# First layer of a four-layer graph network: one copy instruction in place of two, and another order of turns

## The chip, the cores and the metric

The kernel runs on one core of one Trainium2 chip. The metric is the device time of one execution in microseconds (us), which is the time that the core needs from its first to its last instruction and what lies around it.

## The reference

Eight graphs of 1024 nodes with 256 features each pass through four layers, one after the other. Each layer is a kind of attention over the 1024 x 1024 adjacency of the graph. Only the first layer is touched by the change:

```
feat_proj = feats @ fc_w.T + fc_b
q = feat_proj @ q_w.T + q_b                      # one number for each node
k = feat_proj @ k_w.T + k_b                      # one number for each node
logits = q + transpose(k)                        # 1024 x 1024
masked = logits + (1.0 - adj) * -1e9
masked = where(masked >= 0, masked, 0.01 * masked)   # leaky
out = softmax(masked, axis=-1) @ feat_proj + feats
```

The second layer is an attention with one head and a layer norm. The third and the fourth are attentions with eight heads, and the fourth has a feed-forward part with a GELU behind it. All numbers are float32 where this text has to do with them.

## The kernel before

One engine program is written by hand for each engine, and semaphores order the engines among each other. All engines loop over the eight graphs (seven in a hardware loop, the last one unrolled behind it). Within one graph the stages follow each other: first layer, second layer, the two layers with heads, feed-forward. The end of a graph's feed-forward part also holds the beginning of the next graph's first layer.

The first layer goes over T = 8 tiles of 128 rows. For tile t:

- GpSimd (`penalties`, L1311) writes (adj - 1) * 1e9 into `scores[t % 3]`. It waits until TensorE has transposed tile t - 3, because the ring has three buffers.
- VectorE adds the row of keys and takes the row maximum (L1076), and makes the negated maximum with three small instructions (L1078, L1080, L1082). This step is called the maxima here.
- ScalarE makes `slack[t % 2]`, 0.01 times the scores with a bias (L824). This is the slack pass.
- VectorE takes the larger of scores + q and slack (L1089). This is the leaky pass.
- ScalarE takes the exponential in place and sums the row (L829), and signals `p_ready`.
- TensorE (`attend`) transposes the eight 128 x 128 blocks of the tile into PSUM banks 4 and 5 (L536). I write T(t) for these eight instructions. Both banks belong to one tile, so T(t) waits for the copies of tile t - 1.
- ScalarE copies bank 4 (L780) and VectorE copies bank 5 (L969) into `probs_t[t % 2]`.
- TensorE multiplies the copied tile with the values (L546, 16 instructions). I write AV(t) for these. The result lies in bank 6 + t % 2.
- VectorE divides by the row's sum, adds x, and writes `y` (L1095 and L1100). I write y(t) for L1100.

The order of TensorE is T(0), T(1), AV(0), T(2), AV(1), ..., T(7), AV(6), AV(7), both before and after. In its step t VectorE does the maxima of tile t, the leaky pass of tile t - 1, the copy of tile t - 2 and y(t - 3). In its step t ScalarE does the slack pass of tile t, the exponential of tile t - 1 and the copy of tile t - 2. START = 3 of these steps are done ahead, during the feed-forward part of the graph before; they hold three maxima, three slack passes, two leaky passes and two exponentials.

When the first layer is done, TensorE turns `y` (L471) for the second layer's products (L500). The feed-forward part ends with products at L492 and additions of VectorE at L1246.

Of the kernel before, what the change touches and what calls it, by code (L numbers as in the profile page):

```python
# [21 lines left out]
ACT = mybir.ActivationFunctionType  # L22
ALU = mybir.AluOpType
# [4 lines left out]
D = 256  # L28
T = N // P
C = D // P  # L30
HALF = 512
# [55 lines left out]
DVE_STEPS_START = 10  # L87
START = 3

# [8 lines left out]
def build(nc, a, out):  # L98
    B = out.shape[0]
    with ExitStack() as ctx:  # L100
# [3 lines left out]
        def sem(name):  # L104
# [156 lines left out]
        per_graph += [(s, 16 * H) for s in max_row_in] + [(s, 64 * H) for s in o_moved]  # L261
        per_graph += [(s, T) for s in (pen_ready, mask_used, s_done, slack_done, leaky_done, y_ready, g_ready,
                                       e_ready, g3_ready)]
        per_graph += [(s, 2 * T) for s in (s_ready, p_ready, t_done, t_act, t_dve, av_done, av_taken, normal)]
        per_graph += [(s, 2 * H) for s in (max_cast, rows_done, rows_taken, v_ready, o_out)]
# [176 lines left out]
        def _(pe):  # L442
# [84 lines left out]
            def attend(b, layer, t):  # L527

                base = b * 2 * T + layer * T
                if t < T:  # L530
                    pe.wait_ge(p_ready, base + t + 1)

                    pe.wait_ge(t_act, base + t)
                    pe.wait_ge(t_dve, base + t)
                    for k in range(T):
                        last = nc.tensor.transpose(flat[:, 4 * HALF + k * P:4 * HALF + (k + 1) * P],  # L536
                                                   scores[:, t % 3, k * P:(k + 1) * P], ident[:, :])
                    last.then_inc(t_done, 1)
                if t > 0:
                    pe.wait_ge(t_act, base + t)  # L540
                    pe.wait_ge(t_dve, base + t)
# [214 lines left out]
        def _(act):  # L756
# [18 lines left out]
            def copy_probs(b, layer, t):  # L775
# [42 lines left out]
            act.wait_ge(const_made, CONSTS)  # L818
            def layer0(b, steps):

                for t in steps:
                    if t < T:
                        act.wait_ge(s_ready, times(b, 2 * T) + t + 1)
                        nc.scalar.activation(slack[:, t % 2, :], scores[:, t % 3, :], ACT.Identity,  # L824
                                             bias=slack_q[:, t:t + 1], scale=0.01).then_inc(slack_done, 1)
                    if 0 < t <= T:
                        u = t - 1
                        act.wait_ge(leaky_done, times(b, T) + u + 1)
                        nc.scalar.activation(scores[:, u % 3, :], scores[:, u % 3, :], ACT.Exp,  # L829
                                             bias=neg_top[:, u:u + 1], accum_out=denom[:, u:u + 1]).then_inc(p_ready, 1)  # L830
                    if t > START - 1:
                        copy_probs(b, 0, t - 2)

# [14 lines left out]
            def whole(b, final):  # L848

                copy_probs(b, 0, 0)  # L850
                layer0(b, range(START, T + 2))

# [67 lines left out]
                if not final:  # L920
                    layer0((b, 1), range(START))

# [3 lines left out]
            act.sem_inc(act_emptied, N_ACT - emptied_before("proj0", T - 1)[0] - 1)  # L926
            layer0(1, range(START))
            act.wait_ge(weights_in, 16 * len(weight_dmas))
# [6 lines left out]
        def _(dve):  # L935
# [27 lines left out]

            def copy_probs(b, layer, t):

                base = b * 2 * T + layer * T
                dve.wait_ge(t_done, base + t + 1)
# [100 lines left out]

            def layer0(b, steps):

                for t in steps:
                    if t < T:
                        s = scores[:, t % 3, :]
                        dve.wait_ge(pen_ready, times(b, T) + t + 1)
                        dve.sem_inc(passed, 1)
                        then(nc.vector.tensor_tensor_reduce(s, s, key_row[:, :], 1.0, LOWEST, ALU.add, ALU.max,  # L1076
                                                            top[:, t:t + 1]))
                        then(nc.vector.tensor_scalar(top2[:, t:t + 1], top[:, t:t + 1], q_n[:, t:t + 1], None, ALU.add))  # L1078

                        then(nc.vector.scalar_tensor_tensor(top[:, t:t + 1], top2[:, t:t + 1], 0.01, top2[:, t:t + 1],  # L1080
                                                            ALU.mult, ALU.max))
                        nc.vector.tensor_scalar(neg_top[:, t:t + 1], top[:, t:t + 1], -1.0, None, ALU.mult)\  # L1082
                          .then_inc(s_ready, 1)
                    if 0 < t <= T:

                        u = t - 1
                        s = scores[:, u % 3, :]
                        dve.wait_ge(slack_done, times(b, T) + u + 1)
                        nc.vector.scalar_tensor_tensor(s, s, q_n[:, u:u + 1], slack[:, u % 2, :], ALU.add, ALU.max)\  # L1089
                          .then_inc(leaky_done, 1)  # L1090
                    if START - 1 < t <= T + 1:
                        copy_probs(b, 0, t - 2)
                    if t > 2:
                        u = t - 3
                        then(nc.vector.reciprocal(rden[:, u:u + 1], denom[:, u:u + 1]))  # L1095
                        dve.wait_ge(av_done, b * 2 * T + u + 1)
                        if u == 0:
                            dve.wait_ge(stored, b * 64)
                            dve.wait_ge(x_biased, b + 1)
                        nc.vector.scalar_tensor_tensor(y[:, u, :], ps[:, 6 + u % 2, 0:D], rden[:, u:u + 1],  # L1100
                                                       x_in[:, u, :], ALU.mult, ALU.add).then_inc(av_taken, 1)

            def start(b, before):

                wait_all_emptied(dve, before, "proj0", T)
                then(nc.vector.tensor_scalar(slack_q[:, :], q_n[:, :], 0.01, None, ALU.mult))
                layer0(b, range(START))

            def whole(b, final):
                graph[0] = body[0] = b  # L1110
                steps[0] = norms[0] = 0

                copy_probs(b, 0, 0)
                layer0(b, range(START, T + 3))

# [10 lines left out]
                for t in range(T + 3):  # L1126
# [15 lines left out]
                    if 0 < t <= T:  # L1142
                        copy_probs(b, 1, t - 1)
                    if 1 < t <= T + 1:
# [260 lines left out]
```

## Time and profile before

| what | value |
|---|---|
| time, median of 3 runs | 4806.83 us (4800.89 to 4817.36) |
| span of the profiled execution | 4813.5 us |
| its own time | only the span is on record for it, which lies inside the range of the runs |
| TensorE busy | 4350.4 us, 90% |
| VectorE, ScalarE, GpSimd busy | 3470.6, 2036.0, 1891.2 us |
| mean granted clock of TensorE | 0.936 |
| first layer's stage, from T(0) to the first turn | 43.2 to 43.9 us in graphs 2 to 7 |

The span is what the profile's rows cover. The busy share of an engine is an average over all stages; what counts for the change is which wait ends last in the stage of the first layer. Times in the rows are counted from the start of the span.

### The profile page before, as it was taken

Reading aid. Unit: us, or ns where it says so; the run is one execution under the profiler, and the core shown is the slowest. Engines: PE = TensorE matmul, PEld = TensorE weight load, DVE = VectorE, ACT = ScalarE, POOL = GpSimd, SP = SyncE. Lnnn points to the kernel's source line nnn. Section 1 sums busy time; section 2 is a strip of 40 time slices with the busy share of each in tenths; the row PEclk is TensorE's granted clock in tenths of the full one; section 3 lists DMA queues with packets and bytes.
Section 4 is the critical chain, followed back from the end, with each engine's and each line's share of the span. In section 5 each row is a group of like instructions: output and inputs, shape, how many; then the busy total and the mean of one; then the engine's idle time right before and its main releaser. Section 6 shows DMA issues by size and latency. Waiting matters only on the chain.

```text
span 4813.5 us, 60309 instructions
## 1 busy us (share of the span) xinstructions
PE 4350.4 (90%) x16536; PEld 2024.2 (42%) x16536; DVE 3470.6 (72%) x4411; ACT 2036.0 (42%) x3654; POOL 1891.2 (39%) x1064
## 2 busy tenths in 40 slices
PE   7998899988999889998899998998989989899898
PEld 5523265232642336433374333643336432463324
DVE  3798737987379864798648986488854888558893
ACT  3264432544325443354433644235442354423543
POOL 1164601646026450264502645036440364403553
PEclk9999999999999999999999999999999999999999
DMA  3201102011020110201101011010111101111010
GB/s 103 66 18 31 49 19 62 18 31 49 23 59 17 33 47 23 60 16 34 46 28 55 16 34 49 30 53 14 36 47 34 49 14 36 49 35 47 13 36 16
DMA packets 109026, 179.72 MB, mean 37 GB/s; under 512 B 28256, under 2 KB 51040, under 8 KB 108704
## 3 DMA queue, kind: packets, MB, share of 16 engines
q1 hardware_dynamic: 108704, 175.89, 12.7%
q8 instruction: 146, 2.39, 0.2%
q14 instruction: 176, 1.44, 0.1%
HBM read 83.12 MB, written 8.39 MB: 19 GB/s over the span
## 4 chain that ended last, share of the span: by engine, by line
PE 60%; issue 16%; POOL 14%; DVE 7%; ACT 2%; POOLq 0%; DMA 0%; SPq 0%; DVEq 0%; ACTq 0%
PE ps L500 12%; PE ps L604 11%; POOL region_p L1280 9%; PE ps L546 9%; PE ps L492 7%; PE ps L583 6%; PE ps L570 5%; PE ps L694 5%; PE ps L536 2%; DVE row_max L1034 2%; POOL v_head L1274 1%; POOL rstd L1292 1%; DVE region_p L1026 1%; DVE sums_t L1005 1%; POOL y_t L1345 1%
## 5 line engine op out<-in xcount | busy, mean ns | idle before, releaser
L1280 POOL TENSOR_TENSOR region_p<-region_p,mask 128x1024 f32<-128x1024 f32 x512 | 1305.5, 2551 | 728.9 <-ACT region_p L798 728.8
L798 ACT ACTIVATE region_p<-ps 128x512 f32<-128x512 f32 x2048 | 1111.5, 595 | 905.0 <-PE ps L570 903.3
L1034 DVE TENSOR_REDUCE row_max<-ps 128x1 f32<-128x1024 f32 x1024 | 1212.6, 1213 | 42.3 <-PE ps L583 41.1
L604 PE MATMUL ps<-region_p,v_head 128*64 128x512 f32 x4096 | 1131.6, 634 | 73.9 <-POOL region_p L1280 29.7
L1026 DVE TENSOR_TENSOR region_p<-region_p,mask 128x1024 f32<-128x1024 f32 x512 | 772.8, 1512 | 63.5 <-ACT region_p L798 62.9
L583 PE MATMUL ps<-region_k,region_q 96*128 (+1 forms) x2048 | 658.8, 411 | 58.4 <-DVE row_max L1034 53.9
L570 PE MATMUL ps<-region_q,region_k 97*128 (+1 forms) x2048 | 655.8, 400 | 4.0 <-ACT region_p L798 1.1
L1292 POOL TENSOR_TENSOR rstd<-var_eps,minus_half 128x2 f32<-128x2 f32 (+1 forms) x160 | 117.9, 737 | 930.9 <-DVE var_eps L986 930.9
L546 PE MATMUL ps<-values,region_k 128*128 128x256 f32 x2048 | 470.8, 384 | 0.0
L583 PEld LDWEIGHTS ps<-region_k,region_q 96*128 (+1 forms) x2048 | 130.0, 99 | 723.5 <-issue 462.1
L604 PEld LDWEIGHTS ps<-region_p,v_head 128*64 128x64 f32 x4096 | 208.4, 138 | 518.6 <-issue 400.8
L546 PEld LDWEIGHTS ps<-values,region_k 128*128 128x128 f32 x2048 | 386.8, 194 | 49.3
L570 PEld LDWEIGHTS ps<-region_q,region_k 97*128 (+1 forms) x2048 | 197.5, 100 | 434.8 <-ACT region_p L798 207.3
L1274 POOL COPY v_head<-values 128x256 f32 (+1 forms) x128 | 146.6, 1145 | 497.9 <-ACT values L759 497.9
L1311 POOL TENSOR_SCALAR region_p<-mask 128x1024 f32<-128x1024 f32 x64 | 85.2, 1331 | 494.2 <-PE ps L536 472.4
L500 PE MATMUL ps<-y_t,w_q 128*128 128x512 f32 x384 | 208.9, 690 | 65.3 <-ACT y_t L763 19.5
L1005 DVE RECIPROCAL sums_t<-sums_t 128x256 f32<-128x256 f32 (+1 forms) x96 | 216.3, 2267 | 68.6 <-DMA sums_t<-o_raw 68.6
L500 PE MATMUL ps<-y_t,wf 128*128 128x512 f32 x512 | 243.0, 636 | 21.4 <-ACT y_t L763 14.6
L694 PE MATMUL ps<-region_q 128*128 128x512 f32 x512 | 229.7, 594 | 6.4 <-DVE values L1124 6.4
L864 ACT ACTIVATE region_p<-region_p,neg_top 128x1024 f32<-128x1024 f32 x64 | 73.5, 1149 | 341.5 <-DVE neg_top L1140 341.5
L536 PE MATMUL ps<-ident,region_p 128*128 128x128 f32 x1024 | 145.5, 288 | 58.7 <-ACT region_k L780 28.2
L500 PE MATMUL ps<-y_t,w_k 128*128 128x512 f32 x384 | 188.8, 634 | 0.0
(132 smaller groups left out, 4465.4 us busy)
## 6 DMA issues: line engine op xcount, KB each, us to landing
mask<-in_adj SPq DMA_DIRECT2D x64, 512.0 KB, 7.4
mask<-in_adj_t SPq DMA_DIRECT2D x64, 512.0 KB, 3.3
y_t<-o_raw SPq DMA_DIRECT2D x256, 64.0 KB, 2.0
sums_t<-o_raw SPq DMA_DIRECT2D x256, 64.0 KB, 2.0
region_q<-region_p SPq DMA_DIRECT2D x192, 64.0 KB, 2.0
region_k<-region_p SPq DMA_DIRECT2D x192, 64.0 KB, 2.0
region_q<-sums_t SPq DMA_DIRECT2D x192, 64.0 KB, 2.0
region_k<-sums_t SPq DMA_DIRECT2D x192, 64.0 KB, 2.0
```

The source lines that it names most:

```text
L492: last = nc.tensor.matmul(ps[:, bank, j * D:(j + 1) * D], lhs(c, t), rhs[:, c, :], start=(c == 0), stop=(c == tiles - 1))
L500: last = nc.tensor.matmul(ps[:, bank, :], weight[:, c, m * P:(m + 1) * P], y_t[:, c, half * HALF:(half + 1) * HALF], start=(c == 0), stop= ...
L546: last = nc.tensor.matmul(ps[:, 6 + (t - 1) % 2, 0:D], probs_t[:, (t - 1) % 2, k, :], (values0, values)[layer][:, k, :], start=(k == 0), s ...
L570: nc.tensor.matmul(ps[:, 4 + c, :], k_aug[0:AUG, number(h), t * P:(t + 1) * P], q_aug[0:AUG, number(h), c * HALF:(c + 1) * HALF], start=Tr ...
L583: last = nc.tensor.matmul(ps[:, 2 * (t % 2) + c, :], q_aug[0:AUG - 1, number(h), t * P:(t + 1) * P], k_aug[0:AUG - 1, number(h), c * HALF: ...
L604: last = nc.tensor.matmul(ps[64 * c:64 * c + 64, 6 + i, :], v_head[i][:, t, :], probs[:, t % RING, c * HALF:(c + 1) * HALF], start=(t == 0 ...
L694: last = nc.tensor.matmul(ps[:, 2 * (t % 2) + n, :], q_t[:, c, t * P:(t + 1) * P], k_t[:, c, n * HALF:(n + 1) * HALF], start=(c == 0), sto ...
L798: nc.scalar.activation(probs[:, t % RING, c * HALF:(c + 1) * HALF], ps[:, 4 + c, :], ACT.Exp, scale=DK ** -0.5).then_inc(exp_done, 1)
L1005: return nc.vector.reciprocal(sums_t[:, g, cut], sums_t[:, g, cut])
L1026: nc.vector.tensor_tensor(p, p, mask[:, t, :], ALU.mult).then_inc(masked_dve, 1)
L1034: nc.vector.tensor_reduce(row_max[i][:, t:t + 1], flat[:, (t % 2) * N:(t % 2 + 1) * N], AX.X, ALU.max)\
L1280: nc.gpsimd.tensor_tensor(p, p, mask[:, t, :], ALU.mult).then_inc(masked_pool, 1)
```

## The change

ScalarE copies both banks of a transposed tile in one instruction in the first layer, and VectorE copies nothing there. The steps are cut up and ordered anew. In its turn t VectorE now does the leaky pass of tile t + 1, the maxima of tile t + 3, and y(t). In its turn t ScalarE does the copy of tile t, the exponential of tile t + 1 and the slack pass of tile t + 3. What is done ahead now holds three maxima, three slack passes, one leaky pass and one exponential. The order of TensorE stays; it no longer waits for VectorE's copies in this layer. The second layer keeps its two copies.

```diff
                     pe.wait_ge(t_act, base + t)
-                    pe.wait_ge(t_dve, base + t)
+                    if layer:
+                        pe.wait_ge(t_dve, b * T + t)
...
-                nc.scalar.copy(probs_t[:, t % 2, 0:4, :].rearrange("p t q -> p (t q)"), ps[:, 4, :]).then_inc(t_act, 1)
+                n = 1 if layer else 2
+                nc.scalar.copy(probs_t[:, t % 2, 0:4 * n, :].rearrange("p t q -> p (t q)"),
+                               flat[:, 4 * HALF:(4 + n) * HALF]).then_inc(t_act, 1)
...
+            def slack_of(b, t):
+                act.wait_ge(s_ready, times(b, 2 * T) + t + 1)
+                nc.scalar.activation(slack[:, t % 2, :], scores[:, t % 3, :], ACT.Identity,
+                                     bias=slack_q[:, t:t + 1], scale=0.01).then_inc(slack_done, 1)
+
+            def exp_of(b, t):
+                act.wait_ge(leaky_done, times(b, T) + t + 1)
+                nc.scalar.activation(scores[:, t % 3, :], scores[:, t % 3, :], ACT.Exp,
+                                     bias=neg_top[:, t:t + 1], accum_out=denom[:, t:t + 1]).then_inc(p_ready, 1)
+
+            def layer0_start(b):
+
+                for t in range(2):
+                    slack_of(b, t)
+                exp_of(b, 0)
+                slack_of(b, 2)
+
+            def layer0(b):
+
+                for t in range(T):
+                    copy_probs(b, 0, t)
+                    if t + 1 < T:
+                        exp_of(b, t + 1)
+                    if t + 3 < T:
+                        slack_of(b, t + 3)
...
-            def layer0(b, steps):
-
-                for t in steps:
...
-                    if START - 1 < t <= T + 1:
-                        copy_probs(b, 0, t - 2)
-                    if t > 2:
-                        u = t - 3
-                        then(nc.vector.reciprocal(rden[:, u:u + 1], denom[:, u:u + 1]))
-                        dve.wait_ge(av_done, b * 2 * T + u + 1)
...
+            def leaky(b, t):
+                s = scores[:, t % 3, :]
+                dve.wait_ge(slack_done, times(b, T) + t + 1)
+                nc.vector.scalar_tensor_tensor(s, s, q_n[:, t:t + 1], slack[:, t % 2, :], ALU.add, ALU.max)\
+                  .then_inc(leaky_done, 1)
+
+            def layer0(b):
+
+                for t in range(T):
+                    if t + 1 < T:
+                        leaky(b, t + 1)
+                    if t + 3 < T:
+                        masked_top(b, t + 3)
+                    then(nc.vector.reciprocal(rden[:, t:t + 1], denom[:, t:t + 1]))
+                    dve.wait_ge(av_done, b * 2 * T + t + 1)
...
+                    nc.vector.scalar_tensor_tensor(y[:, t, :], ps[:, 6 + t % 2, 0:D], rden[:, t:t + 1],
+                                                   x_in[:, t, :], ALU.mult, ALU.add).then_inc(av_taken, 1)
 
             def start(b, before):
...
-                layer0(b, range(START))
+                masked_top(b, 0)
+                masked_top(b, 1)
+                leaky(b, 0)
+                masked_top(b, 2)
```

`masked_top` (not shown) holds the maxima step with its instructions unchanged.

## Rows read from the trace of the kernel before

**Rows 1.** The page: span, busy time by engine, and the chain by engine.

```profile
span 4813.5 us, 60309 instructions
PE 4350.4 (90%) x16536; PEld 2024.2 (42%) x16536; DVE 3470.6 (72%) x4411; ACT 2036.0 (42%) x3654; POOL 1891.2 (39%) x1064
...
PE 60%; issue 16%; POOL 14%; DVE 7%; ACT 2%; POOLq 0%; DMA 0%; SPq 0%; DVEq 0%; ACTq 0%
```

**Rows 2.** Windows, graphs 4 and 8: length; PE, PEld, DVE, ACT, POOL busy; clock; DMA.

```profile
1838.60:1882.30 43.70, 38.05 (x191) 32.95 (x192) 26.05 (x54) 17.19 (x25) 7.34 (x5) 0.92 0.02 8
...
4220.70:4260.90 40.20, 35.27 (x192) 30.67 (x193) 25.52 (x55) 17.20 (x25) 7.98 (x5) 1.00 0.02 7
```

**Rows 3.** Timeline, graph 4, from the feed-forward part's end to T(2).

```profile
1838.65 0.41 PE L536 MATMUL ps<-ident,region_p 128*128 128x128 f32 x2 [1.18 <-DVE y L1246]
...
1840.54 1.54 PE L536 MATMUL ps<-ident,region_p 128*128 128x128 f32 x6 [1.48 <-issue]
1842.11 0.59 ACT L780 COPY region_k<-ps 128x512 f32<-128x512 f32 x1 [24.75 <-PE ps L536]
1842.11 0.69 DVE L969 COPY region_k<-ps 128x512 f32<-128x512 f32 x1 [3.92 <-PE ps L536]
...
1842.95 1.94 PE L536 MATMUL ps<-ident,region_p 128*128 128x128 f32 x8 [0.88 <-DVE region_k L969]
1843.52 1.22 DVE L1076 CUSTOM_DVE_ANT_0 region_p<-region_p,key_row 128x1024 f32<-128x1024 f32 x1 [0.71 <-POOL region_p L1311]
...
1844.69 4.94 PE L546 MATMUL ps<-values,region_k 128*128 128x256 f32 x16
...
1845.42 1.15 ACT L824 ACTIVATE sums_t<-region_p,slack_q 128x1024 f32<-128x1024 f32 x1 [2.72 <-DVE neg_top L1082]
...
1849.47 1.04 PE L536 MATMUL ps<-ident,region_p 128*128 128x128 f32 x8
```

**Rows 4.** Timeline, graph 4, tiles 3 and 4 in the steady part.

```profile
1855.68 1.06 PE L536 MATMUL ps<-ident,region_p 128*128 128x128 f32 x8 [1.72 <-ACT region_k L780]
...
1856.58 3.62 PE L546 MATMUL ps<-values,region_k 128*128 128x256 f32 x16
...
1860.04 1.04 PE L536 MATMUL ps<-ident,region_p 128*128 128x128 f32 x8
...
1860.31 0.48 DVE L1100 SCALAR_TENSOR_TENSOR y<-ps,rden,x_in 128x256 f32<-128x256 f32 x1 [1.65 <-PE ps L546]
```

**Rows 5.** Timeline, graph 4, the last tiles, up to the second layer's turn.

```profile
1870.68 0.48 DVE L1100 SCALAR_TENSOR_TENSOR y<-ps,rden,x_in 128x256 f32<-128x256 f32 x1 [1.65 <-PE ps L546]
1871.08 1.28 DVE L1089 SCALAR_TENSOR_TENSOR region_p<-region_p,q_n,sums_t 128x1024 f32<-128x1024 f32 x1
...
1872.39 1.15 ACT L829 ACTIVATE region_p<-region_p,neg_top 128x1024 f32<-128x1024 f32 x1 [2.28 <-DVE region_p L1089]
...
1874.74 1.04 PE L536 MATMUL ps<-ident,region_p 128*128 128x128 f32 x8
...
1882.53 1.69 PE L471 MATMUL ps<-ident,y 128*128 128x128 f32 x14
```

**Rows 6.** Timeline, graph 1, exponential of tile 0 and T(0) behind it.

```profile
46.58 1.15 ACT L829 ACTIVATE region_p<-region_p,neg_top 128x1024 f32<-128x1024 f32 x1
...
47.88 0.90 PE L536 MATMUL ps<-ident,region_p 128*128 128x128 f32 x3 [7.32 <-ACT region_p L829]
```

**Rows 7.** Groups by line on ScalarE: count, busy and mean ns, idle before and its releaser.

```profile
L780 ACT COPY region_k<-ps 128x512 f32<-128x512 f32 x128 | 72.7, 568 | 197.0 <-PE ps L536 197.0
```

**Rows 8.** Windows around two idle times of TensorE elsewhere, and behind each.

```profile
1545.20:1548.60 3.40, 0.03 (x2) 0.00 (x0) 1.17 (x2) 0.00 (x0) 3.36 (x1) 0.76 0.00 0
1548.60:1555.00 6.40, 5.46 (x20) 3.57 (x20) 2.36 (x2) 4.36 (x7) 0.00 (x0) 0.59 0.18 44
...
392.80:395.60 2.80, 0.04 (x1) 0.00 (x0) 2.70 (x4) 0.56 (x1) 0.00 (x0) 1.00 0.01 3
395.60:401.00 5.40, 5.37 (x9) 2.36 (x10) 0.75 (x1) 0.69 (x1) 0.00 (x0) 0.68 0.01 3
```

More of the change, by code:

```diff
@@ L87 @@
 DVE_STEPS_START = 10
-START = 3
 def emptied_before(name, i):
@@ L261, in build @@
         per_graph += [(s, 16 * H) for s in max_row_in] + [(s, 64 * H) for s in o_moved]
-        per_graph += [(s, T) for s in (pen_ready, mask_used, s_done, slack_done, leaky_done, y_ready, g_ready,
+        per_graph += [(s, T) for s in (pen_ready, mask_used, s_done, slack_done, leaky_done, t_dve, y_ready, g_ready,
                                        e_ready, g3_ready)]
-        per_graph += [(s, 2 * T) for s in (s_ready, p_ready, t_done, t_act, t_dve, av_done, av_taken, normal)]
+        per_graph += [(s, 2 * T) for s in (s_ready, p_ready, t_done, t_act, av_done, av_taken, normal)]
         per_graph += [(s, 2 * H) for s in (max_cast, rows_done, rows_taken, v_ready, o_out)]
@@ L540, in attend @@
                     pe.wait_ge(t_act, base + t)
-                    pe.wait_ge(t_dve, base + t)
+                    if layer:
+                        pe.wait_ge(t_dve, b * T + t)
                     if layer or t > 2:
@@ L818, in _ @@
             act.wait_ge(const_made, CONSTS)
-            def layer0(b, steps):
-                for t in steps:
[L822 to L831, printed above, removed]
-                        copy_probs(b, 0, t - 2)
+            def slack_of(b, t):
[18 more added lines that the diff above has]
+                        slack_of(b, t + 3)
             def next_keys(b):
@@ L848, in whole @@
             def whole(b, final):
-                copy_probs(b, 0, 0)
-                layer0(b, range(START, T + 2))
+                layer0(b)
                 for half in range(2):
@@ L920, in whole @@
                 if not final:
-                    layer0((b, 1), range(START))
+                    layer0_start((b, 1))
             next_keys(0)
@@ L926, in _ @@
             act.sem_inc(act_emptied, N_ACT - emptied_before("proj0", T - 1)[0] - 1)
-            layer0(1, range(START))
+            layer0_start(1)
             act.wait_ge(weights_in, 16 * len(weight_dmas))
@@ L962, in empty_turn, with copy_probs @@
                                             cols["b" + k][:, 1:2], ALU.mult, ALU.add).then_inc(dve_emptied, 1)
-            def copy_probs(b, layer, t):
-                base = b * 2 * T + layer * T
+            def copy_probs(b, t):
+                base = b * 2 * T + T
                 dve.wait_ge(t_done, base + t + 1)
@@ L1067, in _ @@
             dve.wait_ge(const_made, CONSTS)
[L1069 to L1090, printed above, removed]
-                    if START - 1 < t <= T + 1:
-                        copy_probs(b, 0, t - 2)
-                    if t > 2:
-                        u = t - 3
-                        then(nc.vector.reciprocal(rden[:, u:u + 1], denom[:, u:u + 1]))
-                        dve.wait_ge(av_done, b * 2 * T + u + 1)
[L1097 to L1101, printed above, removed]
@@ new lines, in masked_top @@
+            def masked_top(b, t):
+                s = scores[:, t % 3, :]
+                dve.wait_ge(pen_ready, times(b, T) + t + 1)
+                dve.sem_inc(passed, 1)
+                then(nc.vector.tensor_tensor_reduce(s, s, key_row[:, :], 1.0, LOWEST, ALU.add, ALU.max,
+                                                    top[:, t:t + 1]))
+                then(nc.vector.tensor_scalar(top2[:, t:t + 1], top[:, t:t + 1], q_n[:, t:t + 1], None, ALU.add))
+                then(nc.vector.scalar_tensor_tensor(top[:, t:t + 1], top2[:, t:t + 1], 0.01, top2[:, t:t + 1],
+                                                    ALU.mult, ALU.max))
+                nc.vector.tensor_scalar(neg_top[:, t:t + 1], top[:, t:t + 1], -1.0, None, ALU.mult)\
+                  .then_inc(s_ready, 1)
@@ new lines, in leaky @@
+            def leaky(b, t):
+                s = scores[:, t % 3, :]
+                dve.wait_ge(slack_done, times(b, T) + t + 1)
[9 more added lines that the diff above has]
+                    dve.wait_ge(av_done, b * 2 * T + t + 1)
+                    if t == 0:
+                        dve.wait_ge(stored, b * 64)
+                        dve.wait_ge(x_biased, b + 1)
+                    nc.vector.scalar_tensor_tensor(y[:, t, :], ps[:, 6 + t % 2, 0:D], rden[:, t:t + 1],
+                                                   x_in[:, t, :], ALU.mult, ALU.add).then_inc(av_taken, 1)
@@ L1111, in whole @@
                 steps[0] = norms[0] = 0
-                copy_probs(b, 0, 0)
-                layer0(b, range(START, T + 3))
+                layer0(b)
                 for half in range(2):
```

2 lines of the change are left out of this document (1 added, 1 removed).

## The prediction

> **What bounds the kernel now.** I read the page first. TensorE is busy for 90% of the span and leads the chain of waits, with ScalarE at 2% of it [rows 1]. So what the change does to ScalarE or VectorE counts only where TensorE comes to wait for it. The change touches one stage, so I read the windows of that stage next: from the first transpose to the first turn of the second layer it lasts 43.7 us, with TensorE busy for 38.05 and a granted clock of 0.92, and 40.2 us in the last graph [rows 2].
>
> The timeline then says what paces TensorE inside. In the steady part T(3) begins at 1855.68, AV(2) at 1856.58 and T(4) at 1860.04, with no idle time between them [rows 4]. That is TensorE's floor per tile: 0.90 for a T and 3.46 for an AV, 4.36 us. From T(2) at 1849.47 [rows 3] to T(7) at 1874.74 [rows 5] five tiles take 25.27 us, or 5.05 each. So TensorE loses only 0.7 us per tile now; in some turns it waits for ScalarE's copy, 1.72 us in [rows 4]. The most that a better order can win in these five tiles is 25.27 - 5 x 4.36 = 3.5 us per graph, 28 us over eight. Ahead of them stand T(0), T(1) and AV(0), 10.8 us, where TensorE also has a gap within T(0) that no order of the other engines causes (its reason is "issue") [rows 3].
>
> **What is removed.** VectorE's 64 copies of 0.69 us go [rows 3]. They end TensorE's wait in only some turns (at T(1) they do [rows 3]). ScalarE's copy becomes twice as wide. No row has a 1024-wide copy out of PSUM. Bounds: not less than the 512-wide one, 0.57 us, and not more than two of them, 1.14 [rows 7]; a 1024-wide pass from SBUF takes 1.15 [rows 3]. I take 1.1. It shows once per graph, at T(1). Everywhere else T(t + 1), copy(t + 1) and T(t + 2) have a whole AV between them, so that the copy is hidden by 3.46 us of TensorE work; without this cover it would cost its 1.1 us per tile.
>
> **What is moved, and the wait that comes of it.** This decides. In its new turn t VectorE does leaky(t + 1), the maxima of t + 3, and then waits for AV(t) to write y(t). So leaky(t + 2), the first instruction of the next turn, stands behind the wait for AV(t). TensorE goes T(t + 1), AV(t), T(t + 2), AV(t + 1). T(t + 2) needs the exponential of t + 2, which needs leaky(t + 2). Hence everything from AV(t)'s end to T(t + 2) is serial, with TensorE idle. Before, it was y(t - 3) that stood ahead of leaky(t), and between AV(t - 3) and T(t) TensorE still had T(t - 1) and AV(t - 2) to do. That cover is what goes.
>
> The ring of one tile, each link from a start to the next start:
>
> - AV to y: 1860.31 - 1856.58 = 3.73 us [rows 4].
> - y to the leaky pass directly behind it: 1871.08 - 1870.68 = 0.40 [rows 5].
> - leaky pass to exponential, ScalarE waiting: 1872.39 - 1871.08 = 1.31 [rows 5].
> - exponential to T, TensorE waiting: 47.88 - 46.58 = 1.30 [rows 6].
> - T to AV: 0.90 [rows 4].
>
> The sum is 7.64 us per tile at full clock, against 5.05 now; TensorE works 4.36 of it and idles 3.3.
>
> The other queues fit inside. After leaky(t + 1), 1.3 us, VectorE has the maxima of t + 3, which take 1.9 us (from 1843.52 to the slack pass that they release at 1845.42 [rows 3]), and is then idle until y(t). ScalarE has after exp(t + 1) the slack pass of t + 3 (1.15) and the copy of t + 1 (1.1): counted from the start of leaky(t + 1), slack ends at 4.4, the copy at 5.5, and the next exponential is due at 7.64 + 1.31. GpSimd needs T(t) alone, two turns early. No DMA is issued or moved. The leaky pass and exponential of tile 1, formerly done ahead, fall into the stage. leaky(1) can begin when L1246 ends, which is before T(0) begins, and T(0) takes 3.46 us until it is copied (1842.11 - 1838.65) [rows 3]: hidden. exp(1) stands behind copy(0) and is not hidden.
>
> **The head of the stage.** After these 3.46 us come copy(0) 1.1 and exp(1) to T(1) 1.30: T(1) starts at 5.9, where it was 4.3. It runs at the slow clock, as now, with 1.74 to AV(0), which starts at 7.6. AV(0) took 4.78 to T(2) [rows 3], 1.3 more than 3.46, since its first 2.6 us or so were slow. If the clock comes back at that same moment, 8.7 after T(0)'s start, AV(0) loses 0.5, y(0) is at 7.6 + 3.73 + 0.5 = 11.9 and T(2) 3.0 later, at 14.9. With an idle time of 2.4 us in front of T(1) I expect the slow clock to last longer, with 2.1 us lost in place of 0.5 (how this number comes is below): T(2) at 16.4.
>
> **The clock.** An idle time of 3.3 us in every tile has a price of its own. A 3.4 us idle time of TensorE is followed by a granted clock of 0.59 over 6.4 us; with the 0.76 over the idle time itself that makes 6.9 us at the lower of the two levels (1.2 GHz instead of 2.4), and of the 5.2 us of it that lie behind the idle time half, 2.6 us of work, is lost. Behind 2.8 us of idleness the clock was 0.68 over 5.4 us: 1.7 us lost [rows 8]. No loss occurs too: TensorE idles 1.72 us in [rows 4] and the steady part keeps its full clock. So a tile loses between 0 and 2.6 us; I take 2.1, midway between the two rows, since 3.3 is near their idle times and not near 1.72. A burst of work is 4.36 us long, so at most all of it runs slow: 7.64 + 4.36 = 12.0 per tile. The time per tile that I take is 7.64 + 2.1 = 9.74.
>
> The Trainium skill's page "TensorE: Matmul & The Clock Gate" (section "HAM oscillation — how this bites in real kernels") tells of a kernel whose array falls back to half rate in every round because each round has a wait in it, and counts the cost anew each time. That speaks against this change: by this picture every tile is slowed, as in my likeliest case, and without it the sum is that of the first rival below. No row of this case shows an idle time that comes back in every tile.
>
> **The sum.** T(2) at 16.4; five tiles to T(7), 48.7; from T(7) to the first turn 7.8 now (1882.53 - 1874.74) [rows 5], plus 2.1 for the clock, 9.9. Stage: 75.0 us, against 43.9 between the same two instructions now, so +31.1. The last graph's stage is shorter by its head [rows 2], before and after; I count it like the others. Over eight graphs that is 249 us. The durations are those of the profiled execution, whose span is 4813.5 us: it would come to 5062. The median of the runs lies 6.7 us below that span, and for it the sum is 4807 + 249 = 5056. I say 5050, since the clock's loss is the softest term and can also fail to come in a tile. The stages behind are shifted as they are.
>
> **The rivals.**
>
> *The chain, but the clock holds.* T(2) at 14.9, 5 x 7.64 = 38.2, then 7.8: 60.9, +17.0 per graph, +136: 4943 us. For it: idle times of 1.7 us do no harm now. Against it: [rows 8].
>
> *The clock stays low through the whole stage.* AV(0) loses 3.46, so T(2) at 17.8; 5 x 12.0 = 60; tail 15.6: 93.4, +49.5 per graph: 5203 us. Against it: in [rows 8] it returns within 7 us.
>
> *Faster.* If leaky(t + 2) did not have to wait for AV(t), the relieved engines would let TensorE run at its floor: T(1) comes 1.6 later, the five tiles win 3.5, so -1.9 per graph, 4792 us. Its place is the wait in front of y(t). It decides from the point where the ring is shorter than 4.36, and the ring as added up is 7.64; I would have to have misread the order of VectorE's program. For it: VectorE is rid of 64 x 0.69 = 44 us.
>
> *The wide copy is no gain.* Were the copy across two banks as slow as 2 us, only T(1) would be 0.9 later, 7 us over all. It changes no sign.
>
> **How the numbers follow.** Likeliest case 0.70, its own range 5000 to 5110 (1.3 to 2.6 us lost in each tile, and in head and tail); clock holds 0.17; clock low throughout 0.07; faster 0.04; same 0.02. The range 4935 to 5115 takes in the first rival and leaves out about 2 in 10. A measurement of this kernel can tell about 0.3% (14 us) from no change. Faster by more than that has 0.04, within it 0.02, slower 0.94.
>
> **What would show it.** In the trace after: y(t) directly followed by the leaky pass of t + 2; from T(2) on an idle time of TensorE of about 3.3 us ahead of each T, ended by the exponential; T to T 7.6 us, or with the clock 9 to 10; a granted clock in the stage of 0.7 to 0.8 in place of 0.92; a wide copy of about 1.1 us. A stage of 40 us would prove the ring wrong. One of 61 us at full clock would prove only the clock's term wrong.

## The result and the profile after

The changed kernel takes 4983.47 us (median of 4 runs, 4975.73 to 4988.02) against 4809.47 us for the kernel before (median of 4 runs too). The ratio is 1.036, with a 95% interval of 1.0345 to 1.0377. The forecast was 5050 us, in a range of 4935 to 5115: the direction and the range held, and the forecast was 67 us too high. Three single executions further below (of 5871, 6841 and 7159 us) were in the chip's slower state and are left out of every median and ratio.

The page of the kernel after: span, busy time by engine, and the chain of waits by engine.

```profile
span 4979.4 us, 60157 instructions
...
PE 4391.7 (88%) x16536; PEld 2046.7 (41%) x16536; DVE 3422.4 (69%) x4347; ACT 2063.0 (41%) x3654; POOL 1870.3 (38%) x1064
...
PE 59%; issue 17%; POOL 13%; DVE 7%; ACT 2%; POOLq 0%; DMA 0%; SPq 0%; DVEq 0%; ACTq 0%
```

Beside [rows 1] this page tells almost nothing. VectorE is 48 us less busy and the span is 166 us longer. The shares of the chain hardly move, because the stages are about a tenth of the span. One must go to the stage.

Windows of the kernel after, from T(0) to the first turn of the second layer, graphs 4 and 8 and the sum over all eight:

```profile
1895.30:1961.00 65.70, 43.65 (x193) 35.84 (x194) 20.92 (x47) 21.86 (x27) 5.22 (x5) 0.87 0.02 5
...
4362.70:4426.00 63.30, 42.38 (x192) 35.10 (x193) 20.65 (x47) 21.86 (x27) 5.22 (x5) 0.89 0.01 5
...
sum 523.50, PE 348.43 PEld 287.09 DVE 167.49 ACT 176.19 POOL 42.67; mean PE 43.55 PEld 35.89 DVE 20.94 ACT 22.02 POOL 5.33
```

The stage of graph 4 went from 43.7 us [rows 2] to 65.7. Over eight graphs the stages take 523.5 us where they took 346.1 between the same two instructions, which is 177 us more. VectorE and ScalarE are each busy for only a third of the stage, and TensorE for two thirds: no engine is the bound, so something serial is.

Timeline of the kernel after, graph 4, tiles 2 to 4 (VectorE's maxima and the other queues left out). L1098 is the leaky pass, L1113 is y:

```profile
1910.09 1.33 PE L536 MATMUL ps<-ident,region_p 128*128 128x128 f32 x8 [3.33 <-ACT region_p L829]
...
1911.22 5.10 PE L547 MATMUL ps<-values,region_k 128*128 128x256 f32 x16
...
1916.37 0.48 DVE L1113 SCALAR_TENSOR_TENSOR y<-ps,rden,x_in 128x256 f32<-128x256 f32 x1 [5.75 <-PE ps L547]
1916.77 1.28 DVE L1098 SCALAR_TENSOR_TENSOR region_p<-region_p,q_n,sums_t 128x1024 f32<-128x1024 f32 x1
...
1918.08 1.15 ACT L829 ACTIVATE region_p<-region_p,neg_top 128x1024 f32<-128x1024 f32 x1 [5.45 <-DVE region_p L1098]
...
1919.37 1.09 PE L536 MATMUL ps<-ident,region_p 128*128 128x128 f32 x8 [3.05 <-ACT region_p L829]
...
1920.30 3.62 PE L547 MATMUL ps<-values,region_k 128*128 128x256 f32 x16
...
1923.96 0.48 DVE L1113 SCALAR_TENSOR_TENSOR y<-ps,rden,x_in 128x256 f32<-128x256 f32 x1 [4.07 <-PE ps L547]
1924.36 1.28 DVE L1098 SCALAR_TENSOR_TENSOR region_p<-region_p,q_n,sums_t 128x1024 f32<-128x1024 f32 x1
...
1925.67 1.15 ACT L829 ACTIVATE region_p<-region_p,neg_top 128x1024 f32<-128x1024 f32 x1 [3.77 <-DVE region_p L1098]
...
1926.97 1.16 PE L536 MATMUL ps<-ident,region_p 128*128 128x128 f32 x8 [3.05 <-ACT region_p L829]
```

This is the ring of the prediction, link by link. In the second tile shown: T to AV 0.93, AV to y 3.66, y to leaky 0.40, leaky to exponential 1.31, exponential to T 1.30, in all 7.60 us from T to T. Each wait is ended by the engine that the ring names, and TensorE waits 3.05 us for the exponential. The first tile shown has the same links and takes 9.28: its T and AV ran partly at the lower clock (AV's records last 5.10 us in place of 3.62). In graph 4 the five tiles from T(2) to T(7) take 9.28, 7.60, 9.28, 7.60 and 9.28, 43.0 us in all; over the eight graphs the mean is 8.45 us per tile. Before it was 5.04.

Timeline of the kernel after, graph 4, head of the stage:

```profile
1895.27 0.41 PE L536 MATMUL ps<-ident,region_p 128*128 128x128 f32 x2 [1.18 <-DVE y L1261]
...
1896.93 1.38 PE L536 MATMUL ps<-ident,region_p 128*128 128x128 f32 x6 [1.25 <-issue]
1897.14 1.28 DVE L1098 SCALAR_TENSOR_TENSOR region_p<-region_p,q_n,sums_t 128x1024 f32<-128x1024 f32 x1 [2.32 <-issue]
1898.34 1.01 ACT L782 COPY region_k<-ps 128x1024 f32<-128x1024 f32 x1 [25.49 <-PE ps L536]
...
1899.25 1.15 ACT L829 ACTIVATE region_p<-region_p,neg_top 128x1024 f32<-128x1024 f32 x1
...
1900.55 1.97 PE L536 MATMUL ps<-ident,region_p 128*128 128x128 f32 x8 [2.24 <-ACT region_p L829]
...
1902.31 4.45 PE L547 MATMUL ps<-values,region_k 128*128 128x256 f32 x16
```

The wide copy takes 1.01 us. The leaky pass of tile 1 ends at 1898.42, before it is needed, and T(1) waits for exp(1), which stands behind copy(0). T(1) is 5.28 us after T(0), where it was 4.30. The leaky pass of tile 1 starts only 1.87 us after T(0), not ahead of it as the prediction had it (its idle time has the reason "issue"), and is hidden all the same.

### The profile page after: what moved, and what is told of

It is laid out like the page before. It is cut to its first block, busy times and chain, and to the rows that moved or that the text cites. A ratio compares the mean times of both kernels' runs of the same rounds, so it can differ in the third digit from the quotient of the medians.

```text
span 4979.4 us, 60157 instructions
## 1 busy us (share of the span) xinstructions
PE 4391.7 (88%) x16536; PEld 2046.7 (41%) x16536; DVE 3422.4 (69%) x4347; ACT 2063.0 (41%) x3654; POOL 1870.3 (38%) x1064
## 4 chain that ended last, share of the span: by engine, by line
PE 59%; issue 17%; POOL 13%; DVE 7%; ACT 2%; POOLq 0%; DMA 0%; SPq 0%; DVEq 0%; ACTq 0%
PE ps L499 11%; PE ps L605 11%; PE ps L547 10%; POOL region_p L1295 9%; PE ps L491 7%; PE ps L584 6%; PE ps L571 5%; PE ps L695 4%; PE ps L536 3%; DVE row_max L1047 2%; DVE region_p L1098 1%; POOL v_head L1289 1%; POOL rstd L1307 1%; DVE region_p L1039 1%; DVE sums_t L1018 1%
## 5 line engine op out<-in xcount | busy, mean ns | idle before, releaser
L547 PE MATMUL ps<-values,region_k 128*128 128x256 f32 x2048 | 507.3, 406 | 0.0
L547 PEld LDWEIGHTS ps<-values,region_k 128*128 128x128 f32 x2048 | 413.3, 207 | 60.1
L1326 POOL TENSOR_SCALAR region_p<-mask 128x1024 f32<-128x1024 f32 x64 | 67.7, 1058 | 597.1 <-PE ps L536 570.9
L1113 DVE SCALAR_TENSOR_TENSOR y<-ps,rden,x_in 128x256 f32<-128x256 f32 x64 | 31.0, 484 | 329.5 <-PE ps L547 329.5
L536 PEld LDWEIGHTS ps<-ident,region_p 128*128 128x128 f32 x1024 | 123.9, 150 | 247.4 <-ACT region_p L829 196.6
```

## The experiments

Theory: y's wait for AV(t) stands in front of the leaky pass of t + 2, and the ring through five instructions sets the pace; the clock adds to it. Rivals: the wide copy makes ScalarE the pace; the work of tile 1 inside the stage costs the time.

**y one turn later.** The changed kernel with one edit on VectorE (for tile 0 the lines left out also hold two more waits, the same as before):

```diff
-                for t in range(T):
+                for t in range(T + 1):
                     if t + 1 < T:
                         leaky(b, t + 1)
                     if t + 3 < T:
                         masked_top(b, t + 3)
-                    then(nc.vector.reciprocal(rden[:, t:t + 1], denom[:, t:t + 1]))
-                    dve.wait_ge(av_done, b * 2 * T + t + 1)
+                    if t > 0:
+                        u = t - 1
+                        then(nc.vector.reciprocal(rden[:, u:u + 1], denom[:, u:u + 1]))
+                        dve.wait_ge(av_done, b * 2 * T + u + 1)
...
```

> The changed kernel with one edit on VectorE alone: y(t) is written one turn later, behind the leaky pass of t + 2 and the maxima of t + 4. If the wait for AV(t) in front of that leaky pass is what costs the time, TensorE goes back to its floor: T to T 4.4 us in the steady part, a stage near 42 us, about 4795 us in all. If the wide copy on ScalarE or the work of tile 1 inside the stage were the cause, the time would stay above 4950 us.

Measured: 4771.04 us, 0.9921 of the kernel before (0.9907 to 0.9934). All of the loss is gone, and the kernel is 0.8% faster than before, 24 us below what was expected. The stages did what was expected (327.9 us in sum, 41.0 each); what lies outside them was 25 us shorter than in the kernel before, and that had not been foreseen. Its timeline in graph 4:

```profile
1837.06 1.04 PE L536 MATMUL ps<-ident,region_p 128*128 128x128 f32 x8
...
1837.93 3.62 PE L547 MATMUL ps<-values,region_k 128*128 128x256 f32 x16
1837.96 0.48 DVE L1115 SCALAR_TENSOR_TENSOR y<-ps,rden,x_in 128x256 f32<-128x256 f32 x1
...
1838.36 2.04 DVE L1098 SCALAR_TENSOR_TENSOR region_p<-region_p,q_n,sums_t 128x1024 f32<-128x1024 f32 x1
...
1840.44 1.15 ACT L829 ACTIVATE region_p<-region_p,neg_top 128x1024 f32<-128x1024 f32 x1 [0.61 <-DVE region_p L1098]
...
1841.73 1.09 PE L536 MATMUL ps<-ident,region_p 128*128 128x128 f32 x8 [0.18 <-ACT region_p L829]
```

y now starts without waiting, 0.03 us after the next AV has begun, and the leaky pass runs beneath that AV. TensorE waits for 0.18 us in this tile and not at all in its neighbours. The five tiles take 22.05 us against 43.03 with y in its turn. The same instructions stand in the two kernels; only the place of y(t), with its reciprocal and its wait, differs. This is the theory's ring, shown.

**The wide copy alone.** The kernel before, with ScalarE's copy of both banks and no copy on VectorE, its turns as before:

```diff
-                nc.scalar.copy(probs_t[:, t % 2, 0:4, :].rearrange("p t q -> p (t q)"), ps[:, 4, :]).then_inc(t_act, 1)
+                n = 1 if layer else 2
+                nc.scalar.copy(probs_t[:, t % 2, 0:4 * n, :].rearrange("p t q -> p (t q)"),
+                               flat[:, 4 * HALF:(4 + n) * HALF]).then_inc(t_act, 1)
```

> The kernel before with the wide copy of ScalarE alone, its order of turns kept. By the theory of the wait in front of the leaky pass nothing much happens: ScalarE's copy is 0.45 us longer in the three turns or so of each graph in which TensorE waits for it, 10 us in all, 4820 us. By the theory that the wide copy makes the slowdown it comes near 4980 us.

Measured: 4824.9 us, 1.0034 (1.0023 to 1.0045). The rival falls: with the wide copy alone the kernel is 0.3% slower, not 3.6%. T waits there for a copy that stands behind the exponential. Timeline, graph 4, T(3) and AV(2):

```profile
1855.65 1.06 PE L537 MATMUL ps<-ident,region_p 128*128 128x128 f32 x8 [2.37 <-ACT region_k L783]
...
1856.55 5.30 PE L548 MATMUL ps<-values,region_k 128*128 128x256 f32 x16
```

TensorE waits 2.37 us, against 1.72 in [rows 4], and AV(2) behind it ran partly at the lower clock (5.30 us and not 3.62). The total was foreseen within 5 us, but partly by luck: the stages took 370.1 us in sum, 24 us more than in the kernel before and not 10, and the rest of the kernel was 15 us shorter.

**Tile 1 done ahead again.** The changed kernel with leaky(1) and exp(1) in the part that runs during the feed-forward:

```diff
                 exp_of(b, 0)
                 slack_of(b, 2)
+                exp_of(b, 1)
...
-                    if t + 1 < T:
+                    if 1 < t + 1 < T:
                         exp_of(b, t + 1)
```

and the same on VectorE for the leaky pass.

> The changed kernel with the leaky pass and the exponential of tile 1 done ahead again, in the feed-forward part of the graph before. T(1) no longer waits for that exponential: it comes about 1.2 us earlier, 10 us over eight graphs, 4973 us, and the tiles behind keep their 7.6 to 9.3 us. If this move made the slowdown, the time would fall to near 4810 us.

Measured: 4961.89 us, 1.0318 (1.0303 to 1.0332). It wins 21 us, twice what was expected; 8 of them in the stages (515.8 us in sum against 523.6), where T(1) comes 1.0 us earlier, and the rest elsewhere. The loss stays. The second rival falls.

**TensorE kept busy in the gap.** The changed kernel with products that nobody reads behind AV(0) to AV(5):

```diff
                     last.then_inc(av_done, 1)
+                    if layer == 0 and t < T - 1:
+                        for k in range(6):
+                            nc.tensor.matmul(ps[:, 0, 0:D], ident[:, :], values0[:, k, :], start=True, stop=True)
```

> The changed kernel with six more products of TensorE behind each of AV(0) to AV(5), into a PSUM bank that nobody reads: some 2.6 us of work inside the 3.3 us that TensorE waits. If the falls of the clock in the stage (three or so of 3.4 us per graph) come from this idle time, they go and every tile takes 7.6 us: about 40 us less than the changed kernel, 4943. If the clock is not moved by the gap, the time stays at 4983; if the added work is in the way, it rises.

Measured: 4949.53 us, 1.0291 (1.0272 to 1.0309), 34 us less than the changed kernel (40 less were expected). Its timeline, graph 4 (L552 are the added products), and the window of that stage:

```profile
1909.12 1.09 PE L536 MATMUL ps<-ident,region_p 128*128 128x128 f32 x8 [0.45 <-ACT region_p L832]
...
1910.05 3.62 PE L547 MATMUL ps<-values,region_k 128*128 128x256 f32 x16
...
1913.51 2.75 PE L552 MATMUL ps<-values,ident 128*128 128x256 f32 x12
...
1916.71 1.09 PE L536 MATMUL ps<-ident,region_p 128*128 128x128 f32 x8 [0.46 <-ACT region_p L832]
```

```profile
1887.00:1947.30 60.30, 53.95 (x264) 45.84 (x265) 20.93 (x47) 21.96 (x27) 6.08 (x5) 0.94 0.02 6
```

From T(2) to T(7) every tile now takes 7.60 us (7.66 in graph 8), none 9.28. The granted clock of the stage is 0.94, and what is left of the low level lies in the head. More work on TensorE made the kernel faster, since the work lay in idle time and kept the clock up. So the 7.60 is the ring and the 1.68 on top of it is the clock. The stages sum to 483.7 us, 40 less than the changed kernel's: 34 in the five tiles from T(2) to T(7), 3 behind T(7) and 3 ahead of T(2). Of the 177 us that the stages grew by, 37 were thus the clock's behind T(2). The rest of the kernel was 8 us longer than in the changed kernel.

**The two copies again, in the new order.**

```diff
-                n = 1 if layer else 2
+                n = 1
...
                 for t in range(T):
+                    copy_probs(b, t, 0)
                     if t + 1 < T:
                         leaky(b, t + 1)
```

> The changed kernel, its order of turns kept, with the two shared copies in place of the wide one. The ring that sets the pace holds no copy, so T to T stays at 7.6 to 9.3 us; only T(1) comes 0.4 us earlier, 3 us over eight graphs: about 4980 us. If the wide copy makes the slowdown, near 4810 us.

Measured: 5070.01 us, 1.0553 (1.0538 to 1.0568), 87 us slower than the changed kernel, where 3 us faster was expected. The expectation was wrong: VectorE's copy(t + 1) is the first instruction of its turn and so stands behind y(t) as well, inside the ring. Timeline, graph 4 (L980 is VectorE's copy):

```profile
1953.86 0.48 DVE L1112 SCALAR_TENSOR_TENSOR y<-ps,rden,x_in 128x256 f32<-128x256 f32 x1 [5.84 <-PE ps L545]
1954.26 0.68 DVE L980 COPY region_k<-ps 128x512 f32<-128x512 f32 x1
1954.86 1.28 DVE L1096 SCALAR_TENSOR_TENSOR region_p<-region_p,q_n,sums_t 128x1024 f32<-128x1024 f32 x1
...
1956.17 1.15 ACT L827 ACTIVATE region_p<-region_p,neg_top 128x1024 f32<-128x1024 f32 x1 [6.57 <-DVE region_p L1096]
...
1957.46 1.09 PE L535 MATMUL ps<-ident,region_p 128*128 128x128 f32 x8 [3.73 <-ACT region_p L827]
```

The copy adds 0.60 us, the gap grows to 3.73, and four of the five tiles of graph 4 now also pay 1.7 us to the clock (9.9 to 10.0 us from T to T; the fifth takes 8.28). The wide copy softened the slowdown that the order made.

**The two copies, with y one turn later.** Both edits on the changed kernel together, so that the copies are compared where no ring is in the way:

```diff
+                    if t < T:
+                        copy_probs(b, t, 0)
                     if t + 1 < T:
                         leaky(b, t + 1)
...
+                    if t > 0:
+                        u = t - 1
```

> The changed kernel with y(t) one turn later, and the two copies of bank 4 and bank 5 shared by ScalarE and VectorE again in place of the wide one. VectorE then has 4.5 us of work per tile against TensorE's 4.4, and its copy stands behind its other work: T to T 4.7 us or more, 10 to 30 us slower than with the wide copy, 4780 to 4800 us. If the wide copy brings nothing, 4771 us.

Measured: 4807.58 us, 1.001 (1.0001 to 1.0019), above the 4780 to 4800 that were expected. T to T is 4.7 us in three of the five tiles, as expected, and 4.4 in the others. Against 4771 us with the wide copy, this kernel is 37 us slower, but only 6 of them lie in those five tiles. Another 17 lie ahead of T(2): VectorE's copy(0) now stands ahead of the leaky pass of tile 1, and TensorE waits 3.64 us for T(1) in place of 2.24. The rest lies outside the stages. So the 37 us are the price of two copies at this place in VectorE's turn; a copy placed behind the leaky pass was not tried.

**The ring put into the kernel before.** The kernel before, with y(t - 2) in VectorE's step t in place of y(t - 3):

```diff
                     if t > 2:
-                        u = t - 3
...
+                        write_y(b, t - 2)
...
                 copy_probs(b, 0, 0)
-                layer0(b, range(START, T + 3))
+                write_y(b, 0)
+                layer0(b, range(START, T + 2))
```

`write_y` holds the reciprocal, the wait for AV and the instruction that writes y.

> The kernel before with y(t) one step earlier on VectorE, so that the leaky pass of tile t + 2 stands behind the wait for AV(t) there too, with the maxima (1.9 us) between them. By the theory of the ring, T to T is 7.64 + 1.9 = 9.5 us for four tiles, 7.6 for the last, and T(2) 5 us later: +26 us per graph, 5015 us; with 1.7 us more for the clock in each of six tiles 5095 us. If the place of y does not matter, 4810 us.

Measured: 5144.5 us, 1.0712 (1.0696 to 1.0727), above both expected numbers. Timeline, graph 4:

```profile
1985.48 1.94 PE L536 MATMUL ps<-ident,region_p 128*128 128x128 f32 x8 [5.40 <-ACT region_k L780]
...
1987.22 4.19 PE L546 MATMUL ps<-values,region_k 128*128 128x256 f32 x16
...
1991.52 0.48 DVE L1075 SCALAR_TENSOR_TENSOR y<-ps,rden,x_in 128x256 f32<-128x256 f32 x1 [7.21 <-PE ps L546]
1991.92 1.22 DVE L1085 CUSTOM_DVE_ANT_0 region_p<-region_p,key_row 128x1024 f32<-128x1024 f32 x1
...
1993.69 1.28 DVE L1098 SCALAR_TENSOR_TENSOR region_p<-region_p,q_n,sums_t 128x1024 f32<-128x1024 f32 x1
...
1995.00 1.15 ACT L829 ACTIVATE region_p<-region_p,neg_top 128x1024 f32<-128x1024 f32 x1
...
1996.82 1.94 PE L536 MATMUL ps<-ident,region_p 128*128 128x128 f32 x8 [5.40 <-ACT region_k L780]
```

The ring arises here too, with none of the change's other parts. Two links were missed: T also waits for ScalarE's copy, which stands behind the exponential and adds 0.5 us (exponential to T 1.82, not 1.30), and with 5.4 us of idleness the clock is low for a part of each tile (here T to AV 1.74 and AV to y 4.30). The tile shown takes 11.34 us, and the end of the stage from T(7) on takes 11.0 us in place of 7.8.

**Both at once.** The changed kernel with y one turn later and tile 1 done ahead, by the two edits shown above:

> The changed kernel with y(t) one turn later and with the leaky pass and exponential of tile 1 done ahead. The steady part stays at TensorE's floor of 4.4 us; T(1) comes 1.1 us earlier per graph, which is 9 us over eight: about 4762 us. If the idle time at the stage's head is not bound by that exponential, the time is that of the kernel with y one turn later, 4771 us.

Measured: 4787.57 us, 0.9964 (0.9949 to 0.9978), where 4762 was expected. The stages are shorter, as expected (320.5 us in sum against 327.9 with y one turn later alone), and yet the kernel is slower by 17 us. So I ran both again, side by side on one chip, with two more kernels.

> The changed kernel with y(t) one turn later, once more, beside the kernels below on one chip: 0.992 of the kernel before if its gain outside the first layer's stage (some 20 us, where the clock falls less often) is a property of the kernel; 0.996, the gain of its stage alone, if it was particular to that run.

Measured: 4770.38 us, 0.9927 (0.9908 to 0.9947).

> The kernel with y one turn later and tile 1 done ahead, once more on the same chip as the one above. Its stage is 1 us shorter per graph, but its clock falls more often in the second layer: 0.996 of the kernel before if that is its own, 0.991 if the stage alone decides.

Measured: 4785.48 us, 0.9952 (0.9938 to 0.9967). The difference repeats (15 us; the two intervals overlap a little here, and were apart in the first runs), so it belongs to the kernels. Windows of graph 3: the stage, and from its end to the first scores of the third layer's heads. First y one turn later, in its first run:

```profile
1232.05:1273.41 41.36, 37.47 (x193) 32.70 (x194) 21.94 (x47) 21.57 (x27) 6.81 (x5) 0.92 0.03 8
1273.41:1379.23 105.82, 101.06 (x385) 64.44 (x384) 59.67 (x145) 24.88 (x41) 5.47 (x8) 1.00 0.16 54
```

Then with tile 1 done ahead as well, in its second run:

```profile
1229.90:1270.70 40.80, 37.98 (x193) 33.09 (x194) 20.64 (x46) 20.38 (x25) 7.90 (x5) 0.92 0.03 8
1270.70:1379.34 108.64, 103.88 (x386) 65.53 (x384) 59.66 (x145) 24.87 (x41) 5.47 (x8) 0.97 0.16 53
```

The second stretch holds the same instructions in both, and takes 2.8 us longer where its clock was 0.97 and not 1.00. In that stretch TensorE has one idle time of 2.1 us, behind the last turn of `y`; the next longest is 1.0 us. In graph 3 of the kernel with y one turn later:

```profile
1368.75 1.98 PE L499 MATMUL ps<-y_t,w_q 128*128 128x512 f32 x4 [2.10 <-DVE y_t L971]
```

**That idle time filled.** y late, tile 1 ahead, and four unread products behind the turn:

```diff
                                 turn("y" + n + "_t", i, group)
+                            if layer == 0:
+                                for k in range(4):
+                                    nc.tensor.matmul(ps[:, 4, 0:D], ident[:, :], values0[:, k, :],
+                                                     start=True, stop=True)
```

> The kernel with y one turn later and tile 1 done ahead, and with four products that nobody reads (1.7 us) in TensorE's idle time of 2.1 us ahead of the third layer's products. If that idle time is what lets the clock fall there, the stretch from the second layer's turn to the heads takes 105.8 us in every graph, where it took up to 108.9: about 14 us less over eight graphs, 4774 us. If the falls have another cause, the time stays at 4788 us or rises by the added work.

Measured: 4767.33 us, 0.9918 (0.9902 to 0.9933), 18 us less than without (14 were expected). The same stretch of graph 3:

```profile
1268.03:1373.85 105.82, 102.79 (x393) 65.80 (x392) 59.66 (x145) 24.88 (x41) 5.47 (x8) 1.00 0.17 54
```

It takes 105.8 or 105.9 us in the first seven graphs, and 105.7 in the last. The eight stretches sum to 846.5 us, against 864.3 without the products, which is the whole gain. So the fall of the clock around that idle time is what the second layer paid.

**And the head filled.** As above, with two unread products ahead of T(0) and two behind it:

```diff
+                wait_all_emptied(pe, (b, -1), "proj0", T)
+                for k in range(2):
+                    nc.tensor.matmul(ps[:, 0, 0:D], ident[:, :], values0[:, k, :], start=True, stop=True)
                 pe.wait_ge(ff2_emptied, b * 4)
-                wait_all_emptied(pe, (b, -1), "proj0", T)
                 for t in range(T + 1):
                     attend(b, 0, t)
+                    if t == 0:
...
```

> As the kernel above, and with two more unread products ahead of T(0) and two behind it. If the slow clock at the head of the first layer's stage (6.8 us in each graph) comes from TensorE's short waits there, part of its 3.4 us of lost work per graph comes back: down to 4750 us. If it comes from the gap within T(0), which the added work cannot fill, nothing is won, and the products run slow and in the way: up to 10 us more.

Measured: 4759.88 us, 0.9903 (0.9884 to 0.9921), the fastest kernel of the study. The stages sum to 307.9 us, against 320.6 with the turn alone filled; in some graphs the stage keeps the full clock, in others a low stretch remains. Window of graph 5, from T(0) to the first turn:

```profile
2407.72:2445.71 37.99, 36.16 (x197) 31.49 (x197) 20.82 (x46) 20.22 (x25) 6.61 (x5) 1.00 0.01 2
```

Only half of these 12.7 us is a gain. The gap with the reason "issue", which lay within T(0), now lies ahead of it, among the added products (1.64 us in graph 5), and so outside the stage as it is measured; the rest of the kernel is 6 us longer. The lead over the kernel above is 7 us, and their intervals overlap: this last step is not shown to be a gain.

## Why the prediction was right, and where it was off

1. **The ring was right in place and size.** It was added up to 7.64 us per tile from five links; 7.60 us was measured wherever the clock held, and the place was shown by moving y alone in both directions (-212 us from the changed kernel, +341 us in the kernel before). The forecast fell in its range, but not for the reason held likeliest: that case had a range of its own, 5000 to 5110, and 4983 lies below it. The range held because it also took in the first rival, "the chain, but the clock holds", at 4943. The kernel lies between the two, since the clock fell in only half of the tiles. With the gap filled, the stage of graph 4 took 60.3 us, where that rival's sum was 60.9.

2. **The other queues fit inside**, as said: VectorE and ScalarE idle in every tile, and from T(2) on neither holds TensorE but through the ring. The wide copy took 1.0 us (1.1 taken), and is hidden but at T(1). "The wide copy is no gain" was too low an opinion of it: with y late, the kernel with it is 37 us faster than the one with two copies, though not all of that is the copy's own time.

3. **The head was too long by 1.6 us.** T(1) came 4.5 to 6.2 us after T(0) in graphs 2 to 7 (5.9 taken), and 5.3 in graph 4. T(2) came at 14.8 in graph 4 (16.4 taken): the clock came back at the same moment as before, 8.7 us after T(0), as the lower sum, 14.9, had it. That this sum was met within 0.1 is partly luck: T(1) came 0.6 earlier, and AV(0) lost more at the lower clock than the 0.5 taken (y(0) followed it after 4.7 us in place of 3.73 + 0.5). Of graphs 2 to 8 only graph 6 kept the low clock longer, and there T(2) came at 16.7.

4. **The clock's term is the step that was mis-sized**: "I take 2.1, midway between the two rows". Measured: a fall costs 1.68 us per tile, and it came in 20 of the 40 tiles from T(2) to T(7), so 0.85 on average (8.45 - 7.60). In graph 4 that is 43.0 us for five tiles and not 48.7, and the stage's granted clock was 0.87, not the 0.7 to 0.8 that was named as a sign. The size of one fall was near the lower of the two rows of [rows 8]; that a fall would come in every tile was the error. With the same gap of 3.05 us in front, one tile fell and the next did not; what decides it no run here shows.

5. **The tail's 2.1 us came in two of eight graphs**: 7.8 us from T(7) to the turn, as before, and 9.5 in graphs 3 and 6. In graph 4 it did not come. Together: 75.0 taken, 65.7 measured in graph 4, and the difference of 9.3 is, but for rounding, 1.6 + 5.7 + 2.1 by the three points.

6. **"The stages behind are shifted as they are" was not quite so.** The stages grew by 177 us, the profiled span by 166. From a stage's end to the next one's start the time was 1.3 to 4.3 us shorter in six cases of seven, for the most part since the clock was low for less time around the second layer's idle time (105.8 us in graph 3, against 108.8 before; 9 us over all graphs). This term, which the prediction put at nothing, goes from 0 to 34 us over the kernels of this study (by their spans less their stages), and is as large as the 28 us that a better order could win in the five tiles.

7. **The rivals**: the faster case would have come with the order that the experiment with y one turn later has. The bound of 28 us for a better order was a bound on the five tiles alone; y one turn later gained 39 us, 18 of them in the stages and the rest elsewhere. There the clock explains it: by the mean granted clock of the whole span (0.940 against 0.936) some 22 us less of work was lost at the lower level, and none of that in the stages. The rival's sum, 4792 us, was near for the stages (15 us less taken, 18 measured) and put nothing for the clock elsewhere.

The rule of the Trainium skill's page "TensorE: Matmul & The Clock Gate" (section "HAM oscillation — how this bites in real kernels"), that a wait in each round brings the half rate in each round, agrees in kind. The trace differs in number, and it decides: about every second round fell here, and the filled gap shows the cost, 40 us of the 177.

## What to carry to other kernels

When work is ordered by turns on several in-order engines, follow one tile around: find the first instruction behind each wait, and ask whether the next tile's work on the busy engine hangs on it. A result that nobody needs soon (here y) belongs behind the instruction that feeds the busy engine, even if its input comes a turn earlier. A cheaper copy or less work on a helper engine shows only after that. When a change makes or moves idle times on TensorE of a length behind which its clock has been seen to fall (here 2 to 3 us), measure the stages behind it too: their clock can move by as much as the edit is worth.

## What the runs showed of the hardware that was not expected

- Idle times of 2 to 3 us lie where the clock may fall or not. In the old order an idle time of 1.72 us had no fall behind it; with the wide copy alone it was 2.37 us (and 1.93 us two tiles on, where it had been 1.53), and each graph's stage then had at least one fall more. The same stretch of the second layer took 105.8, 107.4 or 108.7 us in different graphs and kernels, by whether and how long the granted clock fell around one idle time of 2.1 us. A few microseconds' shift of the stage ahead changed which it was. The sum over eight graphs came again in a second run (852.4 and 852.7 us with y one turn later, 859.8 and 864.3 with tile 1 ahead as well), the value of a single graph did not.
- TensorE's work that nobody reads, placed in such an idle time, made the kernel faster: by 34 us in the changed kernel, by 18 us behind the turn.
- Where a graph follows the loop's jump back (graphs 2 to 7), VectorE too starts late: in the changed kernel its first instruction of the stage waited 2.32 to 2.47 us with the reason "issue", as TensorE's gap within T(0) does. In graph 1, and in graph 8, which is unrolled, neither gap is there. What the engines do in that time no run here shows.
